# The first expert tile and the attention stage's last stores: which engine waits for them, where, and where the tile's buffers lie

## The chip, the cores and the metric

The kernel runs on one core of one Trainium2 chip. The metric is the device time of one execution in microseconds (us), the median of several runs. Five engines work side by side, each with a queue of instructions of its own, and meet only through semaphores: TensorE (PE in the profile: matmuls and transposes), VectorE (DVE), ScalarE (ACT: activations and copies), GpSimd (POOL) and SyncE (SP, which here issues DMAs).

## The reference

64 sequences of 93 tokens with 192 features each (16 image patches, 77 text tokens). Three computations follow one another:

```
h = concat(patches @ W_tok + b_tok, layer_norm(sum of 9 table rows))       # embedding
w = layernorm(h) @ w_qkv, 12 heads of 64                                   # attention
Pi = softmax over tokens of temp * sum(w_normed ** 2)
dots = sum over tokens of Pi_norm * w * w
h = h + (-(w * Pi) / (1 + dots)) @ w_out + b_out
z = layernorm(h) through P: 8 sub-spaces of 16                             # experts
per sub-space: the best 4 of 64 experts by z . C, softmax weights over them,
    y = sum of weight * (gelu(z @ W1 + b1) @ W2 + b2)
h = h + gelu(y @ G1 + g1b) @ G2 + g2b
```

The kernel computes all 64 experts of each sub-space and multiplies the hidden values by a gate that is zero for those not chosen.

## The kernel before, in words

**Stages.** Stage 1 embeds and stores h0 to device memory. Stage 2 (attention, and the gates of the experts) goes over 16 units of 372 tokens, in passes: pass_sp, pass_pool, pass_act, pass_dve and pass_pe each list what one engine does of the units that are in flight, written out in order; in pass i unit i is at its beginning and unit i − 3 at its end. Stage 3 (experts) goes over 12 tiles of 496 tokens. Between stages 2 and 3 data goes through device memory: SP stores h1, the three bf16 parts of z (z_parts), the gates, the biases (bias_codes) and the gate scales for each unit, and loads them again by tiles.

**A tile of stage 3.** It has 64 duos; a duo is two hidden products of 128x496, each in one bank of a ring of seven PSUM banks. hidden (line 1696) has TensorE fill a duo's two banks, four matmuls each, as soon as bank_free says that the former user is through. gelu (line 1041) has ScalarE activate them: in place, one bank at a time, for the duos that VectorE gates (DVE_DUOS, 42 of 64), and both at once into one of two SBUF buffers (hid) for those that GpSimd gates (POOL_DUOS: duos 4, 7, 9, 12 and so on). gate_duo (line 793 on GpSimd, 1447 on VectorE) multiplies by the gates gst and writes into the gated space of its quad; a quad is two duos, and there are SPACES = 8 spaces, quad modulo 8. decode (line 1711) lets TensorE multiply a quad's space by w2p and add into the code bank, LAG = 4 quads behind hidden. VectorE's in-place duos hold their banks until they are gated. The sums of a tile are finished (copy_code, add_bias, out1, gelu_out, out2, add_out) at fixed duos of the next tile.

**The turn from stage 2 to stage 3.** One SBUF tensor, arena, holds all stages' buffers; a Carver hands out consecutive words of a row. c1, c2 and c3 start at word 0 for stages 1, 2 and 3; cl starts at LATE = 28200 with the weights of stage 2, over whose first words (w1h, b1h) ct lays gh and bt, the outgoing gates and biases. As c3 lies over c2, stage 3 may write only where stage 2 is done. The helper stage2_over (line 466) waits for the last store of every kind:

```
eng.wait_ge(s_stack, 16 * 9)
wait(eng, s_h1d, 16 * UNITS)
wait(eng, s_zd, 48 * UNITS)
wait(eng, s_gd, 16 * UNITS)
wait(eng, s_bd, 16 * UNITS)
wait(eng, s_rd, 16 * UNITS)
```

It is called on SP (line 607), GpSimd (789), ScalarE (1037) and VectorE (1443), on the last three before anything of stage 3. Then GpSimd sets the last row of y1 to one and s_ones to 2 (791), for which ScalarE waits before its first gelu (1038). TensorE does not call it: it begins hidden of tile 0 after ScalarE's last copies (s_bt, s_rt) and the first half's codes. SP has loaded the codes and gates of tile 0's first half before, the second half's between passes 17 and 18 of stage 2.

The last pass of ScalarE (pass_act(18)) has only z_part2 (line 941, a cast into the second part of z, after which GpSimd's z_part3, line 727, makes the third), copy_bias (920) and copy_scales (926) of unit 15. SP's store_codes waits for z_part3, store_bias and store_scales for the two copies.

Of the kernel before, what the change touches and what calls it, by code (L numbers as in the profile page):

```python
# [27 lines left out]
ACT = mybir.ActivationFunctionType  # L28
# [9 lines left out]
D = 192  # L38
DH2 = D // 2
# [10 lines left out]
UT = UB * N  # L50
ST = 124
# [23 lines left out]
DVE_DUOS = [d for d in range(DUOS) if d not in POOL_DUOS]  # L75
RING = 7
LAG = 4
SPACES = 8
COPY_AFTER = 7
BIAS_AFTER = min(d for d in POOL_DUOS if d > COPY_AFTER)  # L80
OUT1_AT, OUT2_AT = 21, (27, 31)
# [60 lines left out]
def first_of_quad(duo, mine):  # L142

    return duo % 2 == 0 or duo - 1 not in mine
# [9 lines left out]
def build(nc, t):  # L154

    with ExitStack() as ctx:  # L156
# [90 lines left out]
        b1h = cl(32, [3, 512], BF16)  # L247
        wq = cl(DH2, [2, INNER])
        wout = cl(128, [CH, D])
        bout = cl(ST, [D])  # L250
        tempc = cl(128, [1])
        maskh = cl(128, [CH, HEADS])
# [8 lines left out]
        wsq = c2(128, [CH, UT])  # L261
        wpi = c2(128, [CH, UT])
        attended_end = c2.at
        mh2 = c2(ST, [SUB])
        x0 = c2(ST, [SUB, D])
        xr = c2(ST, [SUB, D])
        xb = c2(ST, [SUB, D])
        st = {k: c2(ST, [SUB, 6]) for k in "AG"}
        mv = {k: c2(ST, [SUB, 2]) for k in "AG"}
        ve = {k: c2(ST, [SUB]) for k in "AG"}  # L270
        nb = {k: c2(ST, [SUB]) for k in "AG"}
        rs = {k: c2(ST, [SUB]) for k in "AG"}
        xn = {k: c2(ST, [SUB, D]) for k in "AG"}
        xT = {k: c2(DH2, [2, UT]) for k in "AG"}
        w2pi = c2(128, [CH, UT])
        n2 = c2(128, [CH, UB])
        n2m = c2(128, [CH, UB])
# [14 lines left out]
        dsc = c2(128, [CH, UB])  # L292
        dmi = c2(128, [CH, UB])
        natt = c2(128, [CH, UB])
        h1 = c2(ST, [SUB, D])
        zf = c2(128, [UT])
        zr = c2(128, [UT])
# [21 lines left out]
        zst = c3(ZROWS, [2, PAIRS, TN], BF16)  # L319
        assert c3.at <= attended_end  # L320
        hid = c3(128, [2, 2, TN])
        gated = c3(128, [SPACES, PAIRS, TN])
        comb = c3(128, [TN])
        code = c3(128, [TN])
        y1 = c3(G + 1, [TN])
        bias_t = c3(128, [TN])
        scale_t = c3(128, [TN])
        biased = c3(128, [TN])
        h1t = c3(ST, [TSUB, D])
        outt = c3(ST, [2, TSUB, D])  # L330


        s_w = sem("weights_loaded")
# [80 lines left out]
        def duo_bank(duo, k):  # L414

            return ring[:, bank_of((duo, k)), 0:TN]
# [49 lines left out]
        def stage2_over(eng):  # L466
# [6 lines that stand above are left out]
# [182 lines left out]
        def _(pool):  # L655
# [130 lines left out]
            pool.wait_ge(s_w2l, 16 * (6 + UB + S))  # L786
            for i in range(-2, UNITS + 2):
                pass_pool(i)
            stage2_over(pool)
            pool.wait_ge(s_ones, 1)  # L790
            p_.memset(y1[G:G + 1], 1.0).then_inc(s_ones, 1)

            def gate_duo(tile, duo):

                quad, block, k, j = parts(duo)
                if duo == first_pool[block // EB]:
                    pool.wait_ge(s_gl[block // EB], 32 * (tile + 1))
                if first_of_quad(duo, POOL_DUOS):
                    wait(pool, s_code, QUADS * tile + quad - SPACES + 1)
                pool.wait_ge(s_hid, banks_gelu(tile, duo))  # L800
                p_.tensor_tensor(gated[:, quad % SPACES, j:j + 2], hid[:, POOL_DUOS.index(duo) % 2],  # L801
                                 gst[:, block // EB, j:j + 2], ALU.mult).then_inc(s_pg, 1)

            def add_bias(tile):
# [21 lines left out]
        def _(act):  # L826
# [157 lines left out]
            def pass_act(i):  # L984
                n1, u0, u1, u2, u3 = i + 1, i, i - 1, i - 2, i - 3
                if has(u3):
                    z_part2(u3)
                if has(u0):
                    w_copy(u0, 0)
                    w_copy(u0, 1)  # L990
                if has(u2):
                    scores_copy(u2, 0)
                if has(u0):
                    w_copy(u0, 2)
                    w_copy(u0, 3)
                if has(u2):
                    scores_copy(u2, 1)
                    scores_exp(u2, 0)
                if has(u0):
                    w_copy(u0, 4)  # L1000
                if has(u2):
                    scores_copy(u2, 2)
                if has(u3):
                    copy_bias(u3)
                if has(u2):
                    z_part1(u2)
                if has(u0):
                    w_copy(u0, 5)
                if has(u2):
                    scores_exp(u2, 1)  # L1010
                    scores_exp(u2, 2)
                if has(u3):
                    copy_scales(u3)
                if has(n1):
                    norm("A", n1, x0)
                if has(u2):
                    gates_copy(u2, 0)
                    top4_exp(u2)
                if has(u0):
                    logits_exp(u0)  # L1020
                if has(u2):
                    gates_copy(u2, 1)
                if has(u0):
                    pi_placed(u0)
                if has(u2):
                    gates_copy(u2, 2)
                if has(n1):
                    copy_xT("A", n1)
                if has(u1):
                    norm("G", u1, h1)  # L1030
                    copy_xT("G", u1)
                    z_copy(u1)

            for i in range(-1, UNITS + 3):
                pass_act(i)

            stage2_over(act)
            act.wait_ge(s_ones, 2)
            act.wait_ge(s_w, 64)

# [46 lines left out]
        def _(dve):  # L1087
# [352 lines left out]
            for i in range(-1, UNITS + 3):  # L1440
                pass_dve(i)

            stage2_over(dve)

            first_dve = [min(d for d in DVE_DUOS if d >= DUOS // 2 * o) for o in range(2)]

            def gate_duo(tile, duo):
                quad, block, k, j = parts(duo)
                if duo == first_dve[block // EB]:
                    dve.wait_ge(s_gl[block // EB], 32 * (tile + 1))  # L1450
                if first_of_quad(duo, DVE_DUOS):
                    wait(dve, s_code, QUADS * tile + quad - SPACES + 1)
                for p in range(2):
                    dve.wait_ge(s_hid, banks_gelu(tile, duo, p))
                    v_.tensor_tensor(gated[:, quad % SPACES, j + p], duo_bank(duo, p),  # L1455
                                     gst[:, block // EB, j + p], ALU.mult).then_inc(s_gat, 1)

            def add_out(tile, half, par):
# [30 lines left out]
        def _(pe):  # L1489
# [221 lines left out]
            def decode(tile, quad):  # L1711

                pe.wait_ge(s_gat, dve_gated(tile, 2 * quad + 1))
                pe.wait_ge(s_pg, pool_gated(tile, 2 * quad + 1))
                if quad == 0:
                    wait(pe, s_comb, tile)
                block, k = divmod(quad, KH)
                o, eb = divmod(block, EB)
                for j in range(PAIRS):
                    mm = t_.matmul(code_bank[32 * j:32 * j + 32, 0:TN], w2p[:, chunk(2 * j + o, eb, k)],  # L1720
                                   gated[:, quad % SPACES, j], start=(quad == 0), stop=(quad == QUADS - 1),
                                   skip_group_check=True)
                mm.then_inc(s_code, 1)

# [104 lines left out]
```

## Time and profile before

| | |
|---|---|
| runs shown | 1417.12 us median of 3 (1416.96 to 1417.2) |
| the profiled execution's own time | 1417.62 us |
| its span | 1415.6 us |
| PE busy | 1238.1 us, 87% |
| DVE busy | 1102.1 us, 78% |
| ACT busy | 1092.6 us, 77% |
| POOL busy | 1009.6 us, 71% |
| ACT gelu in place, L1047 | 1008 of mean 695 ns |
| ACT gelu of a duo, L1059 | 252 of mean 1127 ns |
| DVE gate, L1455 | 1008 of mean 667 ns |
| POOL gate, L801 | 264 of mean 2315 ns |

An instruction's duration begins before the one ahead of it has wholly ended (12 DVE gates of 0.67 us stand in 7.06 us), so means don't add up to busy times. Names in the profile are coarse: arena is the one SBUF tensor of all stages, ring the seven banks, code the eighth; gates, z_parts, bias_codes and h_scratch lie in device memory. Line numbers are those of the kernel. "Clock" is the share of TensorE's full 2.4 GHz that was granted; 0.50 is 1.2 GHz.

### The profile page before, as it was taken

How to read it: one execution, taken by the hardware profiler on the slowest of the kernel's cores; microseconds unless marked ns; L12 is line 12 of the kernel's file. 1: busy time of each engine (PE TensorE's matmuls, PEld its weight loads, DVE VectorE, ACT ScalarE, POOL GpSimd, SP SyncE). 2: the span in 40 equal slices, each digit the busy share in tenths (PEclk: the TensorE clock that was granted, in tenths of full speed). 3: DMA queues.
4: the chain of work that ended last, by engine and by line, in shares of the span. 5: the costliest groups of instructions: out<-in, count | busy, mean ns of one | idle time of the engine just before them, and what ended most of it. 6: DMA issues, size and time to landing. Idle time of an engine off the chain costs nothing.

```text
span 1415.6 us, 34238 instructions
## 1 busy us (share of the span) xinstructions
PE 1238.1 (87%) x12232; PEld 621.1 (44%) x12232; DVE 1102.1 (78%) x3359; ACT 1092.6 (77%) x2707; POOL 1009.6 (71%) x735
## 2 busy tenths in 40 slices
PE   3842799999999999856999999999999999999996
PEld 3831465666666666522333333333333333333332
DVE  5574378889888988945888788888888888888884
ACT  0232556777677767437999999999999999999994
POOL 5661356765676566624887888888788888888894
PEclk7965799999999999967999999999999999999997
DMA  9554412222222222133124133222414323232410
GB/s 269 139 116 88 64 33 82 86 67 70 90 76 66 71 92 66 50 107 78 41 58 98 41 80 75 57 63 56 91 43 87 68 65 63 55 78 51 93 38 12
DMA packets 95704, 107.05 MB, mean 76 GB/s; under 512 B 12772, under 2 KB 92668, under 8 KB 95254
## 3 DMA queue, kind: packets, MB, share of 16 engines
q1 hardware_dynamic: 91184, 96.00, 26.5%
q10 hardware_dynamic: 2240, 5.08, 2.1%
q0 software_dynamic: 2112, 3.79, 1.1%
q8 instruction: 98, 1.61, 0.5%
q14 instruction: 70, 0.57, 0.1%
HBM read 67.88 MB, written 33.71 MB: 72 GB/s over the span
## 4 chain that ended last, share of the span: by engine, by line
ACT 24%; PE 19%; DVE 8%; issue 2%; POOL 1%; SPq 0%; DMA 0%; POOLq 0%; DVEq 0%; ACTq 0%
ACT ring L1047 16%; PE ring L1707 9%; PE code L1720 8%; ACT arena L1059 8%; DVE arena L1455 7%; PE ring L1739 2%; PE ring L1730 1%; ACT arena L1063 0%; POOL arena L801 0%; DMA bias_codes<-arena 0%; SPq L586 0%; SPq L591 0%; SPq L552 0%; ACT L1047 0%; POOLq L156 0%
## 5 line engine op out<-in xcount | busy, mean ns | idle before, releaser
L1455 DVE TENSOR_TENSOR arena<-ring,arena 128x496 f32<-128x496 f32 x1008 | 611.4, 667 | 142.9 <-ACT ring L1047 140.2
L801 POOL TENSOR_TENSOR arena<-arena 128x992 f32<-128x992 f32 x264 | 607.6, 2315 | 114.1 <-ACT arena L1059 104.2
L1047 ACT ACTIVATE ring<-ring 128x496 f32<-128x496 f32 x1008 | 545.2, 695 | 10.0 <-PE ring L1707 10.0
L1707 PE MATMUL ring<-arena,w_stack 99*32 99x496 bf16 x6144 | 430.8, 376 | 33.1 <-DVE arena L1455 27.4
L1720 PE MATMUL code<-arena,w_pad 128*32 128x496 f32 x3072 | 389.2, 581 | 3.7 <-ACT arena L1063 3.3
L1707 PEld LDWEIGHTS ring<-arena,w_stack 99*32 99x32 bf16 x6144 | 160.0, 95 | 423.7 <-DVE arena L1455 259.2
L1059 ACT ACTIVATE arena<-ring 128x992 f32<-128x992 f32 x252 | 283.9, 1127 | 3.1 <-POOL arena L801 3.1
L1549 PE MATMUL ring<-arena 96*128 96x372 f32 x384 | 135.3, 490 | 1.6 <-ACT arena L904 0.9
L1720 PEld LDWEIGHTS code<-arena,w_pad 128*32 128x32 f32 x3072 | 96.7, 110 | 54.1 <-DVE arena L1455 17.9
L739 POOL TENSOR_TENSOR arena<-arena 128x372 f32<-128x372 f32 x96 | 91.1, 975 | 35.2 <-DVE arena L1295 35.2
L1549 PEld LDWEIGHTS ring<-arena 96*128 96x128 f32 x384 | 71.8, 194 | 62.4 <-ACT arena L912 15.8
L1598 PE MATMUL ring<-arena 128*128 128x376 f32 x192 | 78.5, 534 | 21.1 <-DVE arena L1290 15.2
L912 ACT ACTIVATE arena<-ring 128x93 f32<-128x93 f32 x384 | 92.1, 279 | 0.0
L734 POOL TENSOR_TENSOR arena<-arena 124x512 f32<-124x512 f32 x48 | 51.9, 1082 | 50.8 <-DVE arena L1227 50.6
L912 ACT ACTIVATION_READ_ACCUMULATOR arena<-ring 128x1 f32 x384 | 86.2, 238 | 0.0
L1227 DVE MAX8 arena<-arena 124x8 f32<-124x64 f32 x384 | 53.2, 211 | 40.7 <-ACT arena L949 40.7
L1238 DVE MATCH_REPLACE8 arena<-arena 124x72 f32<-124x72 f32 x384 | 78.3, 216 | 0.0
L752 POOL TENSOR_TENSOR arena<-arena 124x576 f32<-124x576 f32 x16 | 19.2, 1203 | 82.7 <-DVE arena L1351 81.9
L747 POOL TENSOR_TENSOR arena<-arena 128x372 f32<-128x372 f32 x96 | 74.7, 806 | 2.1 <-DVE arena L1317 2.1
L910 ACT COPY arena<-ring 128x372 f32<-128x372 f32 x96 | 46.8, 487 | 33.9 <-PE ring L1549 33.9
L1617 PE MATMUL code<-arena 128*124 128x192 f32 x384 | 68.9, 330 | 2.8 <-POOL arena L747 2.8
L898 ACT ACTIVATE arena<-arena 124x192 f32<-124x192 f32 x96 | 45.6, 539 | 31.5 <-DVE arena L1220 31.5
(139 smaller groups left out, 1460.7 us busy)
## 6 DMA issues: line engine op xcount, KB each, us to landing
arena<-gates SPq DMA_DIRECT2D x48, 496.0 KB, 6.7
gates<-arena SPq DMA_DIRECT2D x16, 744.0 KB, 11.6
arena<-h_scratch SPq DMA_DIRECT2D x32, 279.0 KB
arena<-z_parts SPq DMA_DIRECT2D x144, 62.0 KB, 2.7
h_scratch<-arena SPq DMA_DIRECT2D x16, 279.0 KB
z_parts<-arena SPq DMA_DIRECT2D x48, 93.0 KB, 2.1
arena<-h_scratch SPq DMA_DIRECT2D x12, 372.0 KB
out_h<-arena SPq DMA_DIRECT2D x12, 372.0 KB
```

The costliest lines, as they stand in the source:

```text
L739: p_.tensor_tensor(w2pi[:, c], wpi[:, c], wv[:, c], ALU.mult).then_inc(s_w2pi, 1)
L747: p_.tensor_tensor(o, o, natt[:, c].unsqueeze(2).to_broadcast([128, UB, N]), ALU.mult).then_inc(s_o, 1)
L801: p_.tensor_tensor(gated[:, quad % SPACES, j:j + 2], hid[:, POOL_DUOS.index(duo) % 2], gst[:, block // EB, j:j + 2], ALU.mult).then_inc(s_ ...
L912: last = a_.activation(wsq[:, c, N * b:N * b + N], src[:, N * b:N * b + N], ACT.Square, accum_out=n2[:, c, b:b + 1])
L1047: a_.activation(product, product, ACT.Gelu_apprx_tanh).then_inc(s_hid, 1)
L1059: a_.activation(to_pool, product, ACT.Gelu_apprx_tanh).then_inc(s_hid, 1)
L1238: last = v_.match_replace(mr[:, s, g], v4[:, s, g], sc[:, s, g], CHOSEN)
L1455: v_.tensor_tensor(gated[:, quad % SPACES, j + p], duo_bank(duo, p), gst[:, block // EB, j + p], ALU.mult).then_inc(s_gat, 1)
L1549: mm = t_.matmul(o, wq[:, h, 128 * c:128 * c + 128], xT["A"][:, h], start=(h == 0), stop=(h == 1))
L1598: t_.matmul(pair0[:, c % 2, 0:UB * (N + 1)], headsel[:, c], pis.rearrange("p b n -> p (b n)"), start=True, stop=True).then_inc(s_pb, 1)
L1707: mm = t_.matmul(bank[32 * q:32 * q + 32], w1s[:, x + 32 * q:x + 32 * q + 32], zst[:, o, j + p], start=True, stop=True)
L1720: mm = t_.matmul(code_bank[32 * j:32 * j + 32, 0:TN], w2p[:, chunk(2 * j + o, eb, k)], gated[:, quad % SPACES, j], start=(quad == 0), stop ...
```

## The change

- SPACES stays 8, but the gated spaces are eight separate pieces of the arena, spaces[0] to spaces[7]. EARLY_SPACES = 4 of them, for quads 0 to 3, lie where buffers of stage 2 die early: one in the region up to natt, two over the attention weights (wq, wout and what of w1h and b1h gh and bt leave), one behind the end of cl. The four others lie behind outt. comb, code, y1 and biased move into the early region.
- In stage 2, mh2 and the tiles of the second norm (k = "G") move behind natt; all that lay between moves down. The order of the instructions is the same.
- GpSimd and VectorE call stage2_over before their first gate of duo 8 or later (FIRST_LATE) in tile 0: GpSimd at duo 9, VectorE at duo 8.
- ScalarE does not call stage2_over. GpSimd's memset of y1's last row waits for z_part3 of all units (s_z3) instead.
- ScalarE runs a gelu on one element of psm ahead of its last pass, so that the activation table is loaded there.

```diff
-SPACES = 8
+SPACES, EARLY_SPACES = 8, 4
+FIRST_LATE = 2 * EARLY_SPACES
...
         wout = cl(128, [CH, D])
+        cl_weights_end = cl.at
...
         attended_end = c2.at
-        mh2 = c2(ST, [SUB])
-        x0 = c2(ST, [SUB, D])
-        xr = c2(ST, [SUB, D])
-        xb = c2(ST, [SUB, D])
-        st = {k: c2(ST, [SUB, 6]) for k in "AG"}
...
-        xT = {k: c2(DH2, [2, UT]) for k in "AG"}
+        st, mv, ve, nb, rs, xn, xT = {}, {}, {}, {}, {}, {}, {}
+
+        def norm_tiles(k):
+            st[k] = c2(ST, [SUB, 6])
...
+            xT[k] = c2(DH2, [2, UT])
+
+        x0 = c2(ST, [SUB, D])
+        xr = c2(ST, [SUB, D])
+        xb = c2(ST, [SUB, D])
+        norm_tiles("A")
         w2pi = c2(128, [CH, UT])
...
         natt = c2(128, [CH, UB])
+        attention_end = c2.at
+        mh2 = c2(ST, [SUB])
+        norm_tiles("G")
...
         hid = c3(128, [2, 2, TN])
-        gated = c3(128, [SPACES, PAIRS, TN])
         comb = c3(128, [TN])
         code = c3(128, [TN])
         y1 = c3(G + 1, [TN])
+        biased = c3(128, [TN])
+        space0 = c3(128, [PAIRS, TN])
+        assert c3.at <= attention_end
         bias_t = c3(128, [TN])
         scale_t = c3(128, [TN])
-        biased = c3(128, [TN])
         h1t = c3(ST, [TSUB, D])
         outt = c3(ST, [2, TSUB, D])
+        late_spaces = [c3(128, [PAIRS, TN]) for _ in range(SPACES - EARLY_SPACES)]
+        assert c3.at <= LATE
+        cg = Carver(ct.at, cl_weights_end)
+        space1, space2 = cg(128, [PAIRS, TN]), cg(128, [PAIRS, TN])
+        ce = Carver(cl.at)
+        space3 = ce(128, [PAIRS, TN])
+        spaces = [space0, space1, space2, space3] + late_spaces
...
             for i in range(-2, UNITS + 2):
                 pass_pool(i)
-            stage2_over(pool)
             pool.wait_ge(s_ones, 1)
+            pool.wait_ge(s_z3, UNITS)
             p_.memset(y1[G:G + 1], 1.0).then_inc(s_ones, 1)
...
+                if tile == 0 and duo == min(d for d in POOL_DUOS if d >= FIRST_LATE):
+                    stage2_over(pool)
...
-                p_.tensor_tensor(gated[:, quad % SPACES, j:j + 2], hid[:, POOL_DUOS.index(duo) % 2],
+                p_.tensor_tensor(spaces[quad % SPACES][:, j:j + 2], hid[:, POOL_DUOS.index(duo) % 2],
...
-            for i in range(-1, UNITS + 3):
+            for i in range(-1, UNITS + 2):
                 pass_act(i)
-
-            stage2_over(act)
+            a_.activation(psm[0:1], psm[0:1], ACT.Gelu_apprx_tanh)
+            pass_act(UNITS + 2)
+
             act.wait_ge(s_ones, 2)
...
-            stage2_over(dve)
-
...
+                if tile == 0 and duo == min(d for d in DVE_DUOS if d >= FIRST_LATE):
+                    stage2_over(dve)
...
-                    v_.tensor_tensor(gated[:, quad % SPACES, j + p], duo_bank(duo, p),
+                    v_.tensor_tensor(spaces[quad % SPACES][:, j + p], duo_bank(duo, p),
...
-                                   gated[:, quad % SPACES, j], start=(quad == 0), stop=(quad == QUADS - 1),
+                                   spaces[quad % SPACES][:, j], start=(quad == 0), stop=(quad == QUADS - 1),
```

## Rows read from the trace of the kernel before

**Rows 1.** The page's slices: busy tenths of the span in 40 equal slices.

```profile
ACT  0232556777677767437999999999999999999994
```

**Rows 2.** The view of waits, 595 to 665: total us, times, longest us.

```profile
POOL arena L791 <- DMA bias_codes<-arena: 11.7, 1, 11.7
```

**Rows 3.** The chain of waits, 632 to 651: start us, us, what (SPq, POOLq: queues).

```profile
639.45 0.60 SPq L552
...
641.08 5.22 DMA bias_codes<-arena
...
646.33 0.04 POOLq L104
...
646.62 0.51 POOL arena L791
...
647.37 1.28 ACT L1047
...
648.67 0.58 ACT ring L1047
```

**Rows 4.** Timeline of ScalarE: start us, us, instruction, [idle before <-releaser].

```profile
632.98 0.57 ACT L981 COPY arena<-ring 128x496 f32<-128x496 f32 x1 [1.84 <-PE ring L1605]
633.45 0.50 ACT L943 CAST arena<-arena 128x372 bf16<-128x372 f32 x1
635.47 0.47 ACT L924 COPY arena<-ring 128x372 f32<-128x372 f32 x1 [1.51 <-PE ring L1557]
635.83 0.25 ACT L929 COPY arena<-ring 24x124 f32<-24x124 f32 x1
...
648.67 3.90 ACT L1047 ACTIVATE ring<-ring 128x496 f32<-128x496 f32 x8
...
659.99 1.02 ACT L1059 ACTIVATE arena<-ring 128x992 f32<-128x992 f32 x1
```

**Rows 5.** Timeline of TensorE's matmuls.

```profile
635.00 0.38 PE L1563 MATMUL ring<-ident,arena 124*24 124x124 f32 x1
636.18 3.09 PE L1707 MATMUL ring<-arena,w_stack 99*32 99x496 bf16 x28 [0.79 <-ACT arena L924]
650.09 6.74 PE L1707 MATMUL ring<-arena,w_stack 99*32 99x496 bf16 x52 [10.83 <-DVE arena L1455]
...
658.51 1.00 PE L1720 MATMUL code<-arena,w_pad 128*32 128x496 f32 x8
```

**Rows 6.** ScalarE's table loads, by line: count | busy, mean ns | idle before.

```profile
L841 ACT ACT_TABLE_LOAD x1 | 1.3, 1283 | 0.8 <-PEq L1819 0.8
L1047 ACT ACT_TABLE_LOAD x1 | 1.3, 1283 | 11.3 <-POOL arena L791 11.3
```

**Rows 7.** Timeline of GpSimd.

```profile
634.03 0.84 POOL L729 TENSOR_TENSOR arena<-arena 128x372 bf16<-128x372 f32 x1 [4.00 <-ACT arena L943]
...
656.36 7.04 POOL L801 TENSOR_TENSOR arena<-arena 128x992 f32<-128x992 f32 x3 [0.45 <-ACT arena L1059]
```

**Rows 8.** Timeline of VectorE.

```profile
656.79 1.26 DVE L1455 TENSOR_TENSOR arena<-ring,arena 128x496 f32<-128x496 f32 x2 [0.36 <-ACT ring L1047]
658.70 2.42 DVE L1455 TENSOR_TENSOR arena<-ring,arena 128x496 f32<-128x496 f32 x4 [0.66 <-ACT ring L1047]
661.52 2.42 DVE L1455 TENSOR_TENSOR arena<-ring,arena 128x496 f32<-128x496 f32 x4 [0.39 <-ACT ring L1047]
```

**Rows 9.** Stretches: from:to us; busy us of PE, PEld, DVE, ACT, POOL; clock, DMA, GB/s.

```profile
654.00:656.00 2.00, 2.00 (x24) 0.70 (x24) 2.00 (x5) 2.00 (x4) 1.91 (x1) 0.50 0.19 68
656.00:658.00 2.00, 2.00 (x26) 0.69 (x24) 1.64 (x3) 2.00 (x4) 1.64 (x1) 0.74 0.00 0
578.00:579.00 1.00, 0.00 (x0) 0.00 (x0) 0.94 (x7) 0.95 (x4) 1.00 (x1) 1.00 0.13 27
```

**Rows 10.** The page's costliest groups: GpSimd's gate and its product into w2pi.

```profile
L801 POOL TENSOR_TENSOR arena<-arena 128x992 f32<-128x992 f32 x264 | 607.6, 2315 | 114.1 <-ACT arena L1059 104.2
...
L739 POOL TENSOR_TENSOR arena<-arena 128x372 f32<-128x372 f32 x96 | 91.1, 975 | 35.2 <-DVE arena L1295 35.2
```

More of the change, by code:

```diff
@@ L263, in build @@
         attended_end = c2.at
-        mh2 = c2(ST, [SUB])
+        st, mv, ve, nb, rs, xn, xT = {}, {}, {}, {}, {}, {}, {}
+        def norm_tiles(k):
+            st[k] = c2(ST, [SUB, 6])
+            mv[k] = c2(ST, [SUB, 2])
+            ve[k] = c2(ST, [SUB])
+            nb[k] = c2(ST, [SUB])
+            rs[k] = c2(ST, [SUB])
+            xn[k] = c2(ST, [SUB, D])
+            xT[k] = c2(DH2, [2, UT])
         x0 = c2(ST, [SUB, D])
@@ L267, in build @@
         xb = c2(ST, [SUB, D])
-        st = {k: c2(ST, [SUB, 6]) for k in "AG"}
[L269 to L273, printed above, removed]
-        xT = {k: c2(DH2, [2, UT]) for k in "AG"}
+        norm_tiles("A")
         w2pi = c2(128, [CH, UT])
@@ L325, in build @@
         y1 = c3(G + 1, [TN])
+        biased = c3(128, [TN])
+        space0 = c3(128, [PAIRS, TN])
+        assert c3.at <= attention_end
         bias_t = c3(128, [TN])
         scale_t = c3(128, [TN])
-        biased = c3(128, [TN])
         h1t = c3(ST, [TSUB, D])
         outt = c3(ST, [2, TSUB, D])
+        late_spaces = [c3(128, [PAIRS, TN]) for _ in range(SPACES - EARLY_SPACES)]
[5 more added lines that the diff above has]
+        spaces = [space0, space1, space2, space3] + late_spaces
+        assert len(spaces) == SPACES
         s_w = sem("weights_loaded")
```

## The prediction

> **What bounds the kernel now.** I read the page's slices first: the scalar engine's row holds at nine tenths from the twentieth slice on, and dips to 4 and 3 in the two slices where the attention stage ends [rows 1]. So the expert stage goes at the pace of its gelus, and a microsecond by which their row begins sooner is one off the end, unless something later in that row stops it. The view of waits over that dip then names the largest wait in which nothing at all is computed: the pool engine's 11.7 us before its memset of y1's last row, ended by the landing of a store to bias_codes [rows 2]. The chain of waits tells the rest in order: that store is issued at 641.08 and lands at 646.30; pool's memset runs 646.62 to 647.13; the scalar engine, which waited for the memset, loads gelu's table from 647.37 for 1.28 us; the first gelu begins at 648.67 [rows 3]. By the timelines the scalar engine's last copy of the attention stage had begun at 635.83, 0.25 us long [rows 4], and TensorE had filled all seven banks of the ring from 636.18, in 3.09 us [rows 5]. The first tile's input was there 10 us before anyone took it up.
>
> The profiled execution took 1417.62 us, 2.02 more than its span of 1415.60, and 0.5 more than the median 1417.12. I work in span times and take the saving off the median.
>
> **The change part by part.**
>
> *Scalar engine: wait dropped, table ahead.* stage2_over goes; what is left before the first gelu is the memset (s_ones at 2) and a filled bank. The table load moves ahead of the last pass, behind the last gates copy, which begins at 632.98 and takes 0.57, to 633.55. In the last pass only copies remain, and the trace has two table loads in all, the second just ahead of the first gelu [rows 6], though code copies come after it in each tile; so I count no reload. The load takes 1.28, to 634.83. The one-element gelu is bounded by nothing below and by the 0.25 of the smallest copy above [rows 4]; I take 0.2, nearest to that row, as it has the same fixed cost. The cast z_part2, which began at 633.45, now begins at 635.05 and with its 0.50 [rows 4] ends at 635.55: 1.6 us later. Who waits for it: pool's z_part3, then the store of codes. That store waited on SP's queue until 639.45 [rows 3], so it loses nothing. copy_bias stood at 635.47 because TensorE's transpose of the scales, begun at 635.00, took 0.38 [rows 4, 5]; it stays there, with copy_scales behind it, and so TensorE still starts at 636.18.
>
> *Pool: memset without the stores.* z_part3 began 0.08 us after z_part2's end in the profile (633.95 to 634.03) and took 0.84 [rows 4, 7]. So now 635.63 to 636.47; the memset waits for it, 0.08 again, and takes 0.51 [rows 3]: 636.55 to 637.06. From the memset's end to the table load were 0.24 us [rows 3]; with the load gone I give the gelu the same.
>
> *First gelu.* At 637.30. The other thing that it needs, a bank, is filled by 636.18 + 3.09/7 = 636.62, so pool's memset comes last. Against 648.67 that is **11.4 us** earlier: 10.1 of waiting and 1.3 of table load. From below: if z_part2 were not delayed at all, the memset would end 1.6 sooner and the bank would decide, at about 636.72 with the 0.10 that lay between copy_scales' end and TensorE's start [rows 4, 5]; that is a gain of 11.9. From above: see the second rival.
>
> *The six waits, moved to duo 8 (vector) and duo 9 (pool).* They add some 0.04 each on the queue, as pool's step at 646.33 shows [rows 3], and they pass when the stores have landed. The SP queue's order up to there is as before, and its issue times depend on the gates copy, which is not moved; so I leave the landing at 646.30 and let the vector engine begin duo 8 at 646.5. Undelayed it would begin at 656.79 − 11.37 = 645.42 [rows 8]: 1.1 us late. Behind the waiting instruction on the vector engine stand duos 8, 10, 11 and so on; for them waits TensorE, which wants the banks back, and through it the gelus. Duo 8 is two operations of 0.63: done at 647.76. Duo 10 was due at 658.70 − 11.37 = 647.33, so it is 0.4 late, and its group takes 2.42, to 650.18; the next group was due at 661.52 − 11.37 = 650.15 [rows 8]. The idle gaps before these groups (0.66, 0.39) eat the delay. On pool duo 7 is begun at 656.36 − 11.37 = 644.99 and takes 2.35 as a third of its row [rows 7], so duo 9 was not due before 647.34 and waits for nothing. TensorE: the second bank of duo 8 is that of the first half of duo 12, free at 647.8; between lies the decode of quad 1, 1.00 at the full clock [rows 5], so duo 12 is ready at about 648.8 where its gelu was due at 659.99 − 11.37 = 648.62 [rows 4]. A stall of 0.2, bounded by 0 and by the whole 1.1 (no gap eats it). I take 0.2, for the vector engine's gaps are read from rows of just these groups.
>
> *Clock.* TensorE was at its lower level (0.50, 1.2 GHz) when it resumed at 650.09, and the granted clock rose within 656 to 658, after some 6.5 us of matmuls paced by the vector engine [rows 5, 9]. After the change the same pacing follows directly on the seven banks, with no pause: busy from 636.18 on, so I expect the rise by about 643, ahead of the first decode. The short stop near 647 (under 1 us) need not undo it: in 578 to 579 TensorE stood still at a granted 1.00 [rows 9].
>
> *Arena.* Times of operations on moved tiles I leave as they are; what speaks against is the third rival. The attention stage itself I count at nothing: the same instructions in the same order but for mh2's address. The loads of the first tile's first half stand on SP's queue ahead of all this and are untouched; SP's later loads wait for the same landing.
>
> Sum: 11.4 − 0.2 = 11.2; span 1415.6 − 11.2 = 1404.4; median 1417.1 − 11.2 = **1405.9 us**. Its own range, from the bounds (11.9 − 0 and 11.4 − 1.1): 1405.2 to 1406.8.
>
> **The rivals.**
> 1. *The clock is low when decoding begins* (it does not rise by 643, or falls at the stop near 647). At half clock a quad's 16 hidden matmuls take 3.09 × 16/28 = 1.77, its decode up to 2.0 (twice 1.00), together 3.8 [rows 5], against four gelus at 3.90/8 × 4 = 1.95 [rows 4]: 1.8 us lost per quad. One more stretch of 6.5 us [rows 5, 9] holds 1.7 quads: 3.1 lost, 1409.0. For it: the pattern of stops is new, and the clock was low ahead of it [rows 9]. Against: the trace shows it rising under this same pacing.
> 2. *The first gelu comes later*: the scalar engine does not take the cast up straight after the load, or loads a table once more. In rows, one more table load of 1.28 puts the gelu at 638.6; duo 8 is then due at 646.7, after the landing, and the 0.2 falls away: gain 10.1, 1407.0. Against: after the load at 647.37 the gelu followed within 0.02 [rows 3]; but the engine had been empty before it, whereas now a copy is in flight. The Trainium skill (ScalarE: Activation LUTs, section "What ACT_TABLE_LOAD costs") gives a drain of about 1.38 us beside a load of 1.28; the load is the trace's 1283 ns, the drain no row here shows, and by it the time would be about 1407.1.
> 3. *Slower: the gate space at an odd word.* Four of eight spaces leave the old block, and the fourth begins, by my count of the sizes, on an odd word (36533). Pool's 128x372 product into w2pi, also an odd word, takes 975 ns or 2.62 per element, the aligned gate 2315/992 = 2.33 [rows 10]: 12% more. Space 3 takes four quads of 32, so per tile 12 vector operations of 0.605 and two on pool of 2.32; at 12% that is 0.87 + 0.56 = 1.4 per tile, 17 over twelve tiles if nothing hides it: 1405.9 + 17 = 1423. It ends slower than before when four fifths of it land on the gelus' path. Against: the shorter product also carries more fixed cost per element, and a quad's four operations would be 0.3 later, less than the vector engine's gaps of 0.39 to 0.66 [rows 8].
> 4. *The wait only moves*: the stores land later than 646.3, or something else holds the first gelus, and half or less of the gain is left, 1411 to 1417.
>
> **How the numbers follow.** Forecast 0.66; clock 0.12; later gelu 0.13; odd word 0.03; wait only moves 0.06. The range takes in the forecast, the later gelu and the low end of the clock's case: 1404.7 to 1408.7, with some 0.15 outside. What a measurement can tell from no change is 0.2%, 2.8 us: faster means under 1414.3. The first three cases and about half of the last are faster: 0.94; the other half is the same, 0.03; slower 0.03.
>
> **What would show it.** In the changed trace: the table load near 633.5, with the cast behind it at 635.0; pool's memset ending near 637.1; the first gelu at 637.3; bias_codes landing near 646.3, with the vector engine idle about 1 us before duo 8, and no gap of the gelus over 0.3 us around duo 12; the granted clock at 1.00 by 645; from there the same 12 tiles, with the same mean times of the gate operations. Wrong if the memset still ends after 640, if gelus pause for a microsecond or more near 647, or if the gate operations' means rise.

## The result and the profile after

| | before | after |
|---|---|---|
| median of 3 runs, us | 1417.12 | 1408.57 (1406.96 to 1408.9) |
| ratio, 95% interval | | 0.9929 [0.9908, 0.995] |
| profiled execution / its span, us | 1417.62 / 1415.6 | 1408.9 / 1406.8 |

8.6 us faster (forecast 11.2), inside the range, close to its upper end. The wait has gone from where it stood. In the page's slices, of some 35 us each, the dip at the turn reads 5, 3, 8 where [rows 1] has 4, 3, 7; the wait of 11.7 us stood almost wholly in the last of these three; the two deeper ones belong to the attention stage's last passes and are still there:

```profile
ACT  0232557677767776538999999999999999999994
```

ScalarE's timeline (start, us, instruction, idle before) answers to [rows 4]. The load follows the gates copy at once and the cast follows the load; GpSimd's memset, for which the first gelu waits 0.96 us, is now done at 638.31. GpSimd's rows stand behind ScalarE's. Where the row of gelus ran on without a gap in the kernel before, there are now two, of 0.81 and 0.69, both ahead of gelus whose banks TensorE had not filled:

```profile
634.29 0.57 ACT L1001 COPY arena<-ring 128x496 f32<-128x496 f32 x1 [1.83 <-PE ring L1626]
634.88 1.28 ACT L1056 ACT_TABLE_LOAD   x1
636.18 0.20 ACT L1056 ACTIVATE arena<-arena 1x1 f32<-1x1 f32 x1
636.28 0.48 ACT L963 CAST arena<-arena 128x372 bf16<-128x372 f32 x1
...
638.35 3.90 ACT L1068 ACTIVATE ring<-ring 128x496 f32<-128x496 f32 x8 [0.96 <-POOL arena L809]
642.08 1.08 ACT L1080 ACTIVATE arena<-ring 128x992 f32<-128x992 f32 x1
...
647.56 1.68 ACT L1068 ACTIVATE ring<-ring 128x496 f32<-128x496 f32 x3
650.05 0.57 ACT L1068 ACTIVATE ring<-ring 128x496 f32<-128x496 f32 x1 [0.81 <-PE ring L1728]
651.30 1.00 ACT L1080 ACTIVATE arena<-ring 128x992 f32<-128x992 f32 x1 [0.69 <-PE ring L1728]
```

```profile
636.85 0.84 POOL L747 TENSOR_TENSOR arena<-arena 128x372 bf16<-128x372 f32 x1 [5.50 <-ACT arena L963]
637.81 0.50 POOL L809 MEMSET arena<- 1x496 f32 x1
```

Why TensorE had not filled them stands in VectorE's timeline, SP's and its own, shown here in this order. VectorE is through duo 6 at 646.09 and stands 2.79 us before duo 8, until 648.87; SP, which waits for the same six semaphores, goes on at 648.70; TensorE stands 2.19 us until VectorE has given a bank of duo 8 back:

```profile
639.02 7.07 DVE L1476 TENSOR_TENSOR arena<-ring,arena 128x496 f32<-128x496 f32 x12 [5.47 <-ACT ring L1068]
648.87 3.58 DVE L1476 TENSOR_TENSOR arena<-ring,arena 128x496 f32<-128x496 f32 x6 [2.79 <-ACT ring L1068]
652.81 2.42 DVE L1476 TENSOR_TENSOR arena<-ring,arena 128x496 f32<-128x496 f32 x4 [0.35 <-ACT ring L1068]
```

```profile
634.89 0.37 SPq L574 DMA_DIRECT2D gates<-arena  x1
...
638.82 2.57 SPq L609 DMA_DIRECT2D arena<-gates  x2
641.43 1.60 SPq L570 DMA_DIRECT2D z_parts<-arena  x3
643.07 0.49 SPq L578 DMA_DIRECT2D bias_codes<-arena  x1
...
648.70 0.27 SPq L634 DMA_DIRECT2D arena<-h_scratch  x1
```

```profile
637.49 4.39 PE L1728 MATMUL ring<-arena,w_stack 99*32 99x496 bf16 x44 [0.79 <-ACT arena L944]
...
645.78 1.01 PE L1741 MATMUL code<-arena,w_pad 128*32 128x496 f32 x8
...
649.60 0.39 PE L1728 MATMUL ring<-arena,w_stack 99*32 99x496 bf16 x4 [2.19 <-DVE arena L1476]
649.82 1.01 PE L1741 MATMUL code<-arena,w_pad 128*32 128x496 f32 x8
```

I cut each execution at marks that the timelines give: the start of the last gates copy (where the attention stage ends, before anything that the change touches at the turn), the first gelu, and the code copy of tile 0, one tile later. From that copy on both kernels keep time to the tenth: 62.37 us from the first code copy to the second before, 62.38 after, and 699.5 and 699.4 us from the first code copy to the end. (In the profiles of the experiments this last stretch took 698.4 to 699.5 us, so a difference of a microsecond behind the code copy is not an effect of the change.)

| | before | after | difference |
|---|---|---|---|
| last gates copy begins | 632.98 | 634.29 | +1.31 |
| to the first gelu | 15.69 | 4.06 | −11.63 |
| to tile 0's code copy | 67.45 | 69.07 | +1.62 |
| to the end | 699.48 | 699.38 | −0.10 |
| span | 1415.60 | 1406.80 | −8.80 |

Two things are to be explained: 1.6 us lost again inside the first tile, and an attention stage that ended 1.3 us later. Of these 1.3, 0.93 are there already at ScalarE's first copy of transposed inputs, the first work of unit 0 (134.69 before, 135.62 after), ahead of nearly all that the change moves.

### The profile page after: what moved, and what is told of

It reads as the page before. It is cut to its first block, busy times and chain, and to the rows that moved or that the text cites. A ratio compares the mean times of both kernels' runs of the same rounds, so it can differ in the third digit from the quotient of the medians.

```text
span 1406.8 us, 34237 instructions
## 1 busy us (share of the span) xinstructions
PE 1237.8 (88%) x12232; PEld 622.3 (44%) x12232; DVE 1101.4 (78%) x3359; ACT 1093.7 (78%) x2708; POOL 1015.5 (72%) x735
## 4 chain that ended last, share of the span: by engine, by line
ACT 29%; PE 11%; POOL 7%; DVE 4%; issue 4%; POOLq 0%; DVEq 0%; ACTq 0%
ACT ring L1068 19%; ACT arena L1080 9%; POOL arena L821 5%; PE code L1741 5%; PE ring L1728 4%; DVE arena L1476 4%; PE ring L1760 2%; POOL arena L829 1%; POOL arena L827 1%; ACT arena L1076 0%; ACT arena L1088 0%; PE ring L1751 0%; POOLq L157 0%; PE ring L1578 0%; PE ring L1626 0%
## 5 line engine op out<-in xcount | busy, mean ns | idle before, releaser
L821 POOL TENSOR_TENSOR arena<-arena 128x992 f32<-128x992 f32 x264 | 608.4, 2316 | 113.5 <-ACT arena L1080 103.5
L770 POOL TENSOR_TENSOR arena<-arena 124x576 f32<-124x576 f32 x16 | 22.4, 1402 | 82.5 <-DVE arena L1372 81.8
```

The source lines that it names most:

```text
L821: p_.tensor_tensor(spaces[quad % SPACES][:, j:j + 2], hid[:, POOL_DUOS.index(duo) % 2], gst[:, block // EB, j:j + 2], ALU.mult).then_inc(s ...
```

## The experiments

All ran 4 to 12 times, beside runs of the kernel before on the same chip, in three groups on three chips (e0, e1, e2 and e4; f1, f2, e3 and e6; g1 to g4). There the kernel before took 1421.05 (1418.16 to 1423.75), 1419.4 (1417.22 to 1424.16) and 1420.96 (1415.48 to 1427.68), far more spread than in the three runs shown at first; so a microsecond is not told apart by medians, and the marks of the profiled executions, one for each kernel, carry the argument. "Late" is how much later than 8.12 us after the first gelu (its place before the change: 656.79 − 648.67) VectorE began duo 8. "SP goes on" is the landing, as SP shows it; where the stores go first, SP has loads to issue before that wait, and it is an upper bound. "Clock 1.00 from" is the time in us at which the granted clock rose from 0.50 to 1.00, and where it fell again. The last column less 67.45 is what was lost inside the first tile.

| run | median us | ratio, 95% interval | last gates copy | first gelu, after it | SP goes on, after it | late | clock 1.00 from | first gelu to code copy |
|---|---|---|---|---|---|---|---|---|
| before | 1417.12 | | 632.98 | 15.69 | 13.47 | 0 | 657.1 | 67.45 |
| after | 1408.57 | 0.9929 [0.9908, 0.995] | 634.29 | 4.06 | 14.41 | 2.40 | 640.9 | 69.07 |
| e0, after again | 1408.31 | 0.9912 [0.9897, 0.9928] | 634.91 | 4.05 | 14.64 | 2.62 | 650.2 | 69.27 |
| e1, arena alone | 1419.32 | 0.9991 [0.9978, 1.0005] | 635.63 | 16.93 | 14.72 | 0 | 661.1 | 67.56 |
| e2, stores first | 1405.9 | 0.9897 [0.9882, 0.9913] | 631.51 | 4.06 | 11.92 | 0.1 | 647.1 | 68.97 |
| e4, waits at duo 6 | 1411.83 | 0.9936 [0.9921, 0.9951] | 637.26 | 4.05 | 14.58 | 4.1 (duo 6) | 644.2, falls 651.0, 657.8 | 73.43 |
| f1, filled | 1413.18 | 0.9955 [0.9939, 0.9971] | 631.42 | 4.05 | 14.45 | | 650.6 | 73.25 |
| f2, filled, stores first | 1413.22 | 0.9956 [0.9939, 0.9973] | 633.20 | 4.06 | 11.39 | | 651.8 | 72.96 |
| e3, table late | 1407.87 | 0.9915 [0.9898, 0.9932] | 634.26 | 5.21 | 14.74 | 1.58 | 650.0 | 68.48 |
| e6, ScalarE waits | 1417.05 | 0.998 [0.9965, 0.9996] | 631.28 | 14.86 | 14.63 | 0.1 | 655.2 | 67.79 |
| g1, warm, stores first | 1407.64 | 0.9909 [0.9884, 0.9934] | 633.09 | 4.06 | 10.34 | 0.1 | 635.4, falls 642.2, 645.6 | 67.48 |
| g2, warm | 1410.98 | 0.9926 [0.9901, 0.9951] | 637.63 | 4.05 | 13.47 | 1.47 | 642.8 | 68.13 |
| g3, warm, five early | 1408.66 | 0.9917 [0.9893, 0.9941] | 634.53 | 4.05 | 13.23 | 0.1 (duo 10) | 636.7, falls 643.5, 647.0 | 67.44 |
| g4, all | 1407.4 | 0.9901 [0.9876, 0.9925] | 634.86 | 3.61 | 9.40 | 0 | falls 642.4, 649.2 | 68.59 |

My theory at first (A) was that the landing of the last stores decides alone; the rival (B) that the gap is TensorE's own; a third (C) that the new layout makes the attention stage longer.

**e0, the changed kernel again.** 

> The changed kernel once more, to see how its time spreads and to have it on the same chip as the others. Theory A (the landing of the last stores decides: the gelus begin about 10 us sooner, but VectorE stands before duo 8 until the stores have landed, and the end follows the landing at a fixed distance): 1407 to 1409, the first gelu near 637 to 638.5, a gap of 1 to 2 us in the gelus near duos 11 and 12 that is longer where the stores land later. Rival B (the gap comes from TensorE, its clock or its order of decode and hidden, not from the landing): the same gap whatever the landing. Rival C (the moved buffers make the attention stage 1.3 us longer): the last gates copy again near 634.3.

The first gelu and the later landing come again. What I had not looked for stands in TensorE's timeline: the first decode takes 1.87 us here, against 1.01 at 645.78 in the profile after, for the granted clock stayed at 0.50 until 650.2.

```profile
638.11 8.99 PE L1728 MATMUL ring<-arena,w_stack 99*32 99x496 bf16 x80 [0.79 <-ACT arena L944]
646.89 1.87 PE L1741 MATMUL code<-arena,w_pad 128*32 128x496 f32 x8
648.54 1.46 PE L1728 MATMUL ring<-arena,w_stack 99*32 99x496 bf16 x12
...
650.65 1.01 PE L1741 MATMUL code<-arena,w_pad 128*32 128x496 f32 x8
```

**e1, the arena alone.** The new layout with the calls of stage2_over and the table load where they were.

> The new arena with the old waits and the table load where it was. If the layout costs nothing: 1416.7 to 1417.5, the last gates copy within 632.5 to 634.5 as runs differ. Rival C: 1418.4 (1.3 more), or 1417.5 if only the 0.4 that grew inside the attention stage is the layout's. Odd word of the fourth space (rival 3 of the prediction): up to 1434, and gate operations with a longer mean than 667 and 2315 ns.

No difference to the kernel before that can be measured: 0.9991 [0.9978, 1.0005]. Rival C's 1.3 us would be 1.0009, outside the interval, and falls; a layout that costs 0.4 us is not excluded. The last gates copy began at 635.63, later than I expected; with the new layout it began anywhere from 631.3 to 637.6 in the runs of the table, and the 632.98 of before lies within that. In the tiles, 62.36 from copy to copy, and gates of 666 and 2316 ns: the odd word costs nothing that can be measured.

One thing I did not ask. The landing came 14.72 after the gates copy here, and 14.41 to 14.74 in all runs with the new layout and SP's old order but g2 and g3, against 13.47 in the one profile of the kernel before. If the layout held the stores back by 1.25 us, e1, whose first gelu still waits for them, would again take 1.0009 of the kernel before, outside its interval. So the layout is not the likely cause; how far the landing spreads in the kernel before, one profile does not show.

**e2, stores first.**

```diff
             pass_sp(UNITS + 1)
+            pass_sp(UNITS + 2)
             load_codes(0, 1)
             load_gates(0, 1)
-            pass_sp(UNITS + 2)
```

> The changed kernel with SP issuing the last stores of codes, biases and scales ahead of the loads of the second half of tile 0 instead of behind them. Theory A: they land some 3 to 5 us sooner, before duo 8 is due, the gap in the gelus goes, and the time falls by the 1.5 us of the gap: 1.5 below the changed kernel, about 1407. Rival B: the gap stays and so does the time, 1408.5.

The median is 2.4 below e0's, where theory A had 1.5; yet the theory falls here as the only cause, by the profile. The stores have landed by 643.43, where SP goes on, and duo 8 begins in time; the gaps in the gelus stay, 0.78 and 0.61, and 1.52 us are lost in the tile; what makes this execution short is an attention stage that ended at 631.51, 3.4 us before e0's:

```profile
643.79 1.26 DVE L1476 TENSOR_TENSOR arena<-ring,arena 128x496 f32<-128x496 f32 x2 [0.49 <-ACT ring L1068]
```

```profile
645.82 2.00 ACT L1068 ACTIVATE ring<-ring 128x496 f32<-128x496 f32 x4 [0.78 <-PE ring L1728]
648.43 1.00 ACT L1080 ACTIVATE arena<-ring 128x992 f32<-128x992 f32 x1 [0.61 <-PE ring L1728]
```

```profile
643.48 1.87 PE L1741 MATMUL code<-arena,w_pad 128*32 128x496 f32 x8
645.13 1.87 PE L1728 MATMUL ring<-arena,w_stack 99*32 99x496 bf16 x16
646.79 1.17 PE L1741 MATMUL code<-arena,w_pad 128*32 128x496 f32 x8
647.78 1.01 PE L1728 MATMUL ring<-arena,w_stack 99*32 99x496 bf16 x16
```

The first decode and the hidden products behind it take 1.87 each, the next ones 1.17 and 1.01: the clock rose from 0.50 near 647.1, 12.4 us after TensorE had resumed at 634.71. From here on I hold theory A2: a late landing and a low clock each hold back the gelus of duos 10 to 12, and their losses do not add up, as both delay the same banks.

**e4, the waits two duos sooner.** FIRST_LATE = 6 in place of 8.

> The changed kernel with the six waits before duo 6 instead of duo 8 (the arena unchanged). Theory A: the landing is the same, and two duos more are left to do after it, 1.9 us of gelus: 1.9 above the changed kernel, about 1410.4. Rival B: no change, 1408.5.

6.0 us were lost inside the tile, where A had 1.6 + 1.9 = 3.5. This profile is of the slowest of six executions (1416.26); the median is 3.5 above e0's, where A had 1.9. The rest fits the clock once more, though no run separates the two here: behind the gap of 3.53 that the landing makes, two more follow, 1.07 and 1.16, while TensorE works at 0.50.

```profile
653.40 1.00 ACT L1080 ACTIVATE arena<-ring 128x992 f32<-128x992 f32 x1 [3.53 <-PE ring L1728]
655.47 2.00 ACT L1068 ACTIVATE ring<-ring 128x496 f32<-128x496 f32 x4 [1.07 <-PE ring L1728]
658.62 1.00 ACT L1080 ACTIVATE arena<-ring 128x992 f32<-128x992 f32 x1 [1.16 <-PE ring L1728]
```

TensorE, at full clock from 644.2, had next to nothing to do from 648 on, and the clock fell to 0.50 with the stretch from 651 (columns as in [rows 9]):

```profile
644.00:648.00 4.00, 3.10 (x44) 0.80 (x36) 3.88 (x7) 4.00 (x9) 1.74 (x1) 0.98 0.89 201
648.00:651.00 3.00, 0.33 (x4) 0.04 (x4) 0.00 (x0) 1.87 (x4) 0.56 (x1) 1.00 0.93 233
651.00:654.00 3.00, 1.26 (x12) 0.48 (x16) 1.99 (x4) 0.60 (x1) 1.97 (x1) 0.50 0.10 13
654.00:657.00 3.00, 3.00 (x28) 0.96 (x24) 1.36 (x3) 1.93 (x5) 2.62 (x2) 0.50 0.66 164
```

The decode at 653.13 and the next at 656.44 then took 1.87 and 1.71.

**f1 and f2, small matmuls between the first hidden products.**

```diff
+                    if tile == 0 and isinstance(tile, int) and 3 <= duo < 10:
+                        t_.matmul(code_bank[:, 0:180], w1s[:, 0:128], w1s[:, 0:180], start=True, stop=True,
+                                  skip_group_check=True)
                     bank_free(tile, (duo, p))
```

> The changed kernel with 14 small matmuls added (128x180 bf16 into the code bank, results overwritten), one ahead of each bank of duos 3 to 9 of tile 0, so that TensorE works without pauses while VectorE paces it. Theory A2 (two things cut the gelus after duo 9: the landing of the last stores, and a granted clock of 0.50 that rises at one time or another between 3.5 and 12.3 us after TensorE resumes, and makes decode and hidden of quads 4 to 6 take 1.87 instead of 1.01 us): the clock rises before the first decode, what stays is the landing's part; from the last gates copy to the end 771.5 to 772.5, as in the changed kernel's profile (772.51) where the clock had risen early. Rival (the clock has no part): no difference in the gaps and the same 0.50 through the first decode as in the repeated run.

> Stores first and the small matmuls, together. Theory A2: neither the landing nor the clock is left, so the gelus run on without a gap over 0.3 us; from the last gates copy to the end 771.0 (4.06 to the first gelu and the 766.93 that the kernel before takes from there), 1.4 below stores first alone (772.39); time 1404.5 to 1406. Theory A alone (landing only) said that stores first would do it and is out; rival: the gaps come from the order of the early quads and stay at 0.8 and 0.6, total 772.4.

Both failed as experiments. I had counted 180 columns at the low clock as 0.15 us, so that a bank would still be filled in VectorE's 0.585. In f1's timeline a bank takes 0.80 from one to the next: 0.27 from the small matmul's start to that of the hidden products, and 0.53 for these, which take 3.09/7 = 0.44 a bank where seven banks follow one another [rows 5].

```profile
637.22 0.33 PE L1725 MATMUL code<-w_stack 99*128 99x180 bf16 x1
637.49 0.60 PE L1731 MATMUL ring<-arena,w_stack 99*32 99x496 bf16 x4
638.02 0.33 PE L1725 MATMUL code<-w_stack 99*128 99x180 bf16 x1
```

So TensorE itself became the pace of the first duos, 5.5 to 5.8 us were lost, and the clock rose no sooner (16.0 and 15.4 us after hidden began, against 12.1 in e0). They show nothing of A2.

**e3, the table late.** The early gelu left out, the loop over pass_act whole again.

> The changed kernel without the early gelu, so that its table is loaded just ahead of the first gelu again. The first gelu comes 5.0 us after the last gates copy instead of 4.06. Theory A2: where the landing cuts the gelus the end does not move, because duo 8 waits for it anyway (772 to 773 from the last gates copy to the end); if only the start of the gelus decided, 1.0 more than the changed kernel, 773 to 773.5.

The first gelu came 1.15 us later and 1.03 were lost in the tile in place of 1.62 to 1.82. From the gates copy to the code copy that is 73.69, against 73.13 in the profile after and 73.32 in e0's, and 772.1 to the end, within what A2 had. The ratio is 0.9915 beside e0's 0.9912. So while duo 8 waits, the early table is worth 0.4 to 0.6 us in these profiles.

**e6, ScalarE's wait put back.** stage2_over(act) ahead of its wait for s_ones, all else as changed.

> The changed kernel with ScalarE's wait for the last stores put back ahead of its first gelu; the arena, the early table and the moved waits of the other engines stay. Theory A: the first gelu follows the landing by some 0.4 us, 13.7 to 15 us after the last gates copy, so from there to the end 780.5 to 782, about 1.5 under the kernel before (782.62): nearly all of the gain is the gelus begun before the landing. Rival (the gain is the table or the layout): most of the gain stays, under 776.

The first gelu came 14.86 after the gates copy, 0.23 after SP went on, and from the gates copy to the end it is 781.2 (1412.5 − 631.28), as forecast; of the 1.4 less than in the kernel before 0.9 lie behind the first code copy, 0.5 ahead of it. So nearly all of the gain is in the gelus begun ahead of the landing. ScalarE's early table, with GpSimd's memset and the other engines' waits moved, leaves 0.998 [0.9965, 0.9996].

```profile
646.14 3.90 ACT L1069 ACTIVATE ring<-ring 128x496 f32<-128x496 f32 x8 [11.76 <-DMA gate_scales<-arena]
```

**g1, g2 and g3: the clock raised ahead of hidden.** One matmul of fp32 in each of TensorE's pauses at the end of its last pass (400, 500, 360, 160 and 200 columns); g1 with stores first, g3 with a fifth early space in place of comb, code and biased, which moved behind it, out of the early region (EARLY_SPACES = 5, so the waits stand at duo 10).

```diff
+            def warm(u, columns):
+                if u == UNITS - 1 and columns:
+                    t_.matmul(code_bank[:, 0:columns], ident[:], w2p[:].rearrange("p a b -> p (a b)")[:, 0:columns],
+                              start=True, stop=True)
...
                 if has(u3):
+                    warm(u3, 400)
                     gates_transposed(u3, 0)
```

> Five fp32 matmuls (160 to 500 columns into the code bank, results overwritten) put into TensorE's pauses at the end of its last attention pass, so that the clock is at its upper level when hidden begins, and SP's last stores first. Theory A2 (landing and clock each cut the gelus of duos 10 to 12 by 1 to 1.6 us, and not one on top of the other): with both gone, from the first gelu to tile 0's code copy 67.45 to 67.7 us, as in the kernel before (67.45), against 69.07 in the changed kernel and 68.97 with stores first; time about 1.5 below the changed kernel. Rival B (the order of the early quads makes the gap): 69 again.

> The changed kernel with the five fp32 matmuls alone. Theory A2: the landing's part stays, 69.0 us from the first gelu to the code copy, with the clock at 1.00 through the first decode; if only the clock counted, 67.5.

> The five fp32 matmuls, and a fifth early gated space (comb, code and biased moved behind it), so that the six waits stand before duo 10. Theory A2: the landing comes about when duo 10 is due, so of its 1.6 us 0 to 0.4 stay: 67.5 to 67.9 us from the first gelu to the code copy. Rival B: 69.

A2's forecast came in g1 and g3, and rival B's did not: with the landing in time, and the clock back at 1.00 before the second decode, the loss is gone, 67.48 and 67.44. With the landing alone (g2) 0.68 us stay, between A2's 1.5 and the nothing of "only the clock". The landing came sooner, 13.47 after the gates copy, and duo 8 was 1.47 late. Put beside the profile after (2.40 late, 1.62 lost), the first 0.8 of the lateness is absorbed each time and the rest lost one for one; e0's 2.62 and 1.82 fit the same. This reading I made after the runs. The medians show nothing of it: g1's 0.9909 is no lower than stores first alone.

The filling did not hold the clock as meant. In g1 it fell again at 642.2, while VectorE paced TensorE, and was back at 645.6, when the first decode had begun; so too in g3 (643.5 and 647.0):

```profile
642.04 3.25 PE L1738 MATMUL ring<-arena,w_stack 99*32 99x496 bf16 x28 [0.19 <-DVE arena L1476]
645.07 1.27 PE L1751 MATMUL code<-arena,w_pad 128*32 128x496 f32 x8
646.18 1.01 PE L1738 MATMUL ring<-arena,w_stack 99*32 99x496 bf16 x16
647.02 1.00 PE L1751 MATMUL code<-arena,w_pad 128*32 128x496 f32 x8
```

```profile
640.00:642.00 2.00, 1.29 (x16) 0.31 (x12) 2.00 (x5) 2.00 (x5) 0.00 (x0) 1.00 0.56 124
...
643.00:645.00 2.00, 2.00 (x24) 0.77 (x20) 1.89 (x4) 2.00 (x4) 1.56 (x2) 0.50 0.75 169
...
646.00:648.00 2.00, 2.00 (x32) 0.73 (x28) 1.42 (x4) 2.00 (x4) 2.00 (x2) 1.00 1.05 217
```

**g4, all together**, with z_part2 ahead of the early gelu.

> All together, and z_part2 ahead of the early table load: the best version that the runs point to. First gelu 3.7 instead of 4.06 us after the last gates copy, then 67.45 to 67.6 to the code copy: 1.7 to 2 us below the changed kernel, with the attention stage as long as it happens to be, 1404.5 to 1406.5.

The first gelu came at 3.61 and the landing early, but the clock was low from 642.4 to 649.2, and the first decode took 1.87: 1.14 us were lost, and neither the 67.6 nor the 1406.5 that I expected at most was reached. It tests A2 unasked: with the landing in time and the clock low, a part of the loss is back. Stores first and its successors have the lowest ratios (0.9897, 0.9909, 0.9901), yet their intervals overlap that of the changed kernel (0.9912 [0.9897, 0.9928]). On one chip the four runs of stores first (1405.3 to 1407.46) all lie below the four of the changed kernel (1407.6 to 1409.48), which hints at a gain; with an attention stage that ends anywhere within 6 us, so few do not show one.

## Why the prediction was right, and where its sum was off

**The mechanism** was right: begun ahead of the landing, the gelus keep the lead to the end, and from the first code copy on nothing is given back. e6 shows it from the other side. The number is in part luck. By its own bounds the sum had 1405.2 to 1406.8, and 1408.57 lies outside that; the wider range holds it because it kept room for a later gelu and a low clock, and neither is what filled it. In span times the forecast 1404.4 became 1406.8 by −0.26 (first gelu), +1.42 (stop at duo 8), +1.31 (an attention stage that ended later) and −0.10 (the rest). Of the signs named, the gelus' gaps failed: none over 0.3 was forecast, and "a microsecond or more" was to mean wrong; there were two, 0.81 and 0.69. The landing was later than named, too.

**First gelu** (forecast 4.32 after the last gates copy, measured 4.06): the terms held nearly one by one. The load stands at 634.88 where the copy ends at 634.86, and takes 1.28; the small gelu takes 0.20, but the cast followed 0.10 after its start, not its end; from cast to memset it went nearly as laid out, and the gelu followed the memset's end by 0.04, not 0.24. The second rival is out: the gelu stood 0.02 behind the load, with a copy in flight right ahead of it. The Trainium skill (ScalarE: Activation LUTs, "What ACT_TABLE_LOAD costs") adds a drain of about 1.38 us to a load. No run here shows one of that size.

**The stop at duo 8** is the term that was mis-sized: 0.2 forecast and bounded by 1.1, 1.62 measured. The working said "I leave the landing at 646.30" and had duo 8 begin 1.1 late. It was 2.40 late: the gelus came 0.3 sooner than I had them, the landing 0.9 later (SP goes on 14.41 after the gates copy instead of 13.47), and VectorE 0.1 later behind it. Of the later landing 0.67 stood on SP's queue ahead of the stores, where the second half's load of the gates was 2.57 us in being issued (638.82 above) and had been 1.90:

```profile
637.50 1.90 SPq L591 DMA_DIRECT2D arena<-gates  x2
```

The first 0.8 of the lateness was absorbed (0.9 in the working); all beyond it was lost. So the stores did land later, as the fourth rival has it, but most of the gain stayed. That a landing of queued transfers has a spread was in none of my bounds: SP goes on 13.2 to 14.7 after the gates copy in the runs with the old order of SP's queue. What makes that load's issue take 1.26, 1.90 or 2.57 us is not shown.

**The clock** was the first rival with 0.12, and came more often than that. In the five profiles in which the gelus begin ahead of the landing and no matmuls are added, it was low at the first decode in four (e0, e2, e3, and e4, where it had risen and fallen again) and up in one (after). It rose 3.4 us after hidden began in the profile after, but 12.1 (e0) and 12.4 (e2) in others; e2's 1.52 are its price. I had put it at 3.1, for a stretch of 6.5 us of decode and hidden; it rose after some 3.6 of them. As both causes hold back the same banks, e0, which has both, lost 1.82, and not the sum of 1.62 and 1.52.

My ground for a rise by 643 was misread. The working said "the trace shows it rising under this same pacing", from one stretch of one execution. TensorE's first decode, which [rows 5] leaves out, had begun in that stretch, and the rise at 657.1 came 0.5 us behind its start:

```profile
656.62 1.22 PE L1720 MATMUL code<-arena,w_pad 128*32 128x496 f32 x8
```

So the kernel before had not shown the clock rising while VectorE alone paced TensorE. In the other profiles it rose ahead of hidden (g1, g3, g4), while TensorE filled the first seven banks (g2), 0.3 and 0.7 us after it had filled them (after, e4), or else only once a decode had begun. None shows it rising further into that pacing.

**The attention stage**, counted at nothing, is nothing that e1 can measure: the 1.31 by which it ended later in the profile after are best read as a difference between executions. Without them the turn is worth 10.0 us in the two profiles (83.14 to 73.13 from the gates copy to the first code copy), and 9.8 in e0's (73.32).

**The odd word** (third rival) has no price here: the gates' means are 668 and 2316 ns after against 667 and 2315 before.

## What to carry to other kernels

A stage can begin before the last stores of the one before it have landed, if the buffers that it writes first lie over what died early; the lead is kept if the engine that it gives the lead to sets the pace of all that follows. How many buffers must be early is the wait's own length over the time of one buffer, with the landing taken at the late end of its spread. And where TensorE resumes after a pause, its first long stretch of work should be reckoned at half clock too: the first decode took 1.87 us in place of 1.01 in e0, e2, e3 and g4.

## What the runs showed of the hardware

- Where hidden began at a granted 0.50, the clock rose to 1.00 either early, 2.0 (g2), 3.4 (after) and 3.7 us (e4) after hidden began, or not before a decode: in e0, e2 and e3 it stayed at 0.50 while VectorE paced TensorE and rose 12.1 to 12.6 us after hidden began, 2.6 to 3.6 after the first decode had. It fell from 1.00 to 0.50 under that pacing in g1, g3 and g4, and in e4 after 3 us of near standstill.
- A matmul of 99*128 against 99x180 put ahead of each bank's four of 99*32 against 99x496 made a bank take 0.80 us at the low clock, where seven banks in a row take 0.44 each.
- The table load of 1.28 us started 0.02 after the end of the copy ahead of it, and the next activation began 0.02 after the load's end.
- In the executions shown here the attention stage ended anywhere between 631.3 and 637.6 us, and the kernel before took 1415.5 to 1427.7 on the chips of the experiments.
